# Normalising the rows of a mixture layer on GpSimd in place of VectorE

## The reference

```python
x = x + 0.5 * ffn(layernorm(x), ...)
x = x + attn(layernorm(x), ...)
x = x + 0.5 * ffn(layernorm(x), ...)

def layernorm(x, eps=1e-05):
    m = mean(x, axis=-1); v = var(x, axis=-1)
    return (x - m) / sqrt(v + eps)

def ffn(x, ...):                      # 8 experts of width 128, 2 per row, and one shared
    scores = sigmoid(x @ gate_W) * route_scale
    topk_scores, topk_idx = top_k(scores, 2)
    gate_full = ...                   # weights topk_scores / sum, scattered to 8 places
    h = gelu(einsum('bsd,edh->bseh', x, W1) + b1)
    y = einsum('bseh,ehd->bsed', h, W2) + b2
    return einsum('bse,bsed->bsd', gate_full, y) + gelu(x @ Ws1 + bs1) @ Ws2 + bs2
```

## Time and profile before

| | before |
|---|---|
| three timed executions | 2427.08, 2432.66, 2438.47 us, median 2432.66 |
| profiled execution | 2441.92 us, span 2440.1 us |
| TensorE busy | 2388.6 us, 98% of the span |
| VectorE busy | 1865.7 us, 76% |
| ScalarE busy | 1681.6 us, 69% |
| GpSimd busy | 1512.4 us, 62% |
| TensorE in the chain that ended last | 88% of the span |

### The profile page before, as it was taken

The page is one execution under the profiler, slowest core; times in us unless marked ns, Lnnn a source line. Parts: engine busy times, 40 slices in busy tenths (PEclk is TensorE's granted clock), DMA queues, the critical chain, the costliest instruction groups (busy, mean ns, idle before and its releaser), DMA issues.

```text
span 2440.1 us, 46268 instructions
## 1 busy us (share of the span) xinstructions
PE 2388.6 (98%) x14472; PEld 2078.3 (85%) x14472; DVE 1865.7 (76%) x3615; ACT 1681.6 (69%) x2932; POOL 1512.4 (62%) x1536
## 2 busy tenths in 40 slices
PE   8999889999999999999999999999999989999999
PEld 7888778888888888888888888888888879988888
DVE  7887567878888787887878888787887865466675
ACT  4555567878778787887878778787787865443443
POOL 1333267787877878777787777878777754542220
PEclk9999889999999999999999999999999999999999
DMA  4744531213222122321213222122221345432332
GB/s 179 264 162 163 198 113 38 94 47 100 73 74 95 44 86 71 93 95 43 86 57 95 75 67 95 44 86 78 86 95 43 108 157 166 140 115 64 126 130 82
DMA packets 131969, 245.66 MB, mean 101 GB/s; under 512 B 7290, under 2 KB 90132, under 8 KB 120052
## 3 DMA queue, kind: packets, MB, share of 16 engines
q1 hardware_dynamic: 131828, 244.15, 30.7%
HBM read 140.12 MB, written 53.67 MB: 79 GB/s over the span
## 4 chain that ended last, share of the span: by engine, by line
PE 88%; DVE 6%; DMA 2%; issue 1%; ACT 1%; POOL 1%; SPq 0%; DVEq 0%; ACTq 0%; POOLq 0%
PE a_sc L1661 19%; PE a_ov L1697 19%; PE a_tr L1673 18%; PE a_pj L1613 7%; PE a_pj L1620 4%; PE g_acc L963 3%; PE g_hid L921 3%; PE m_proj L2102 3%; PE f_acc L963 2%; PE f_hid L921 2%; PE m_hid L2168 2%; PE m_acc L2139 2%; DMA f_xin<-in_x 1%; DVE f_hp L735 1%; DVE f_gated L730 1%
## 5 line engine op out<-in xcount | busy, mean ns | idle before, releaser
L1569 DVE TENSOR_REDUCE a_nmax<-a_sc 128x1 f32<-128x1024 f32 x512 | 626.7, 1224 | 268.9 <-PE a_sc L1661 265.1
L1412 ACT ACTIVATE a_pT<-a_tr 128x512 fp32r<-128x512 f32 x1024 | 559.7, 596 | 324.2 <-PE a_tr L1673 321.4
L1496 POOL TENSOR_SCALAR a_pr<-a_pr,a_rden 128x1024 f32<-128x1024 f32 x512 | 576.7, 1127 | 294.6 <-DVE a_rden L1574 224.4
L1580 DVE TENSOR_TENSOR a_pT<-a_tr,a_pT 128x512 fp32r<-128x512 f32 x1024 | 650.0, 676 | 15.9 <-ACT a_pT L1412 15.9
L1697 PE MATMUL a_ov<-a_pT,a_v_s 128*128 128x512 f32 x2048 | 598.4, 414 | 3.1 <-DVE a_half L1560 2.0
L1418 ACT ACTIVATE a_pr<-a_sc,a_nmax 128x1024 f32<-128x1024 f32 x512 | 573.9, 1121 | 28.3 <-DVE a_nmax L1569 26.2
L1661 PE MATMUL a_sc<-a_k_s,a_q_s 128*128 128x512 f32 x2048 | 559.3, 395 | 3.5 <-DMA a_k_s<-a_k_s 3.5
L1673 PEld LDWEIGHTS a_tr<-f_ident,a_pr 128*128 128x128 f32 x4096 | 476.6, 140 | 79.7 <-DVE a_pT L1580 6.2
L1673 PE MATMUL a_tr<-f_ident,a_pr 128*128 128x128 f32 x4096 | 537.5, 274 | 1.8 <-DVE a_pT L1580 1.8
L1661 PEld LDWEIGHTS a_sc<-a_k_s,a_q_s 128*128 128x128 f32 x2048 | 378.2, 189 | 79.9 <-DMA a_k_s<-a_k_s 3.7
L1697 PEld LDWEIGHTS a_ov<-a_pT,a_v_s 128*128 128x128 f32 x2048 | 347.0, 189 | 50.5 <-issue 4.7
(11 more groups left out here) (252 smaller groups left out, 3228.4 us busy)
## 6 DMA issues: line engine op xcount, KB each, us to landing
a_z_s<-zT SPq DMA_DIRECT2D x32, 1024.0 KB, 7.7
a_k_s<-a_k_s SPq DMA_DIRECT2D x62, 512.0 KB, 5.6
a_wqk_s<-w_split SPq DMA_DIRECT2D x64, 256.0 KB, 3.2
a_v_s<-a_v_b SPq DMA_DIRECT2D x16, 1024.0 KB, 4.7
att<-a_ao SPq DMA_DIRECT2D x32, 512.0 KB, 2.9
m_in<-att SPq DMA_DIRECT2D x16, 1024.0 KB, 6.1
f_gB<-f_gate_rows SPq DMA_DIRECT2D x12, 1024.0 KB, 5.0
g_gB<-g_gate_rows SPq DMA_DIRECT2D x12, 1024.0 KB, 4.7
```

Of the source, the lines that this page charges most:

```text
L1412: act.activation(pT[:, (u // 4) % 2, 0, 4 * part:4 * part + 4, (u % 4) * P:(u % 4 + 1) * P], tr[:, part].rearrange("p (t q) -> p t q", t=4 ...
L1496: pool.tensor_scalar(pr[:, k % NP], pr[:, k % NP], rden[:, k % NP:k % NP + 1], 1.0, ALU.mult, ALU.mult).then_inc(s["normed"], 1)
L1569: dve.tensor_reduce(nmax[:, k % NP:k % NP + 1], sc[:, k % 2], AX.X, ALU.max, negate=True).then_inc(s["negmax"], 1)
L1580: dve.tensor_tensor(to[:, 1], tr[:, part].rearrange("p (t q) -> p t q", t=4), to[:, 0].bitcast(F32), ALU.subtract).then_inc(s["tr_lo"], 1)
```

## The change

`x_norm` goes from VectorE's stream to GpSimd's, for blocks 1 to 7 of both parts; block 0 stays on VectorE. On GpSimd it stands directly behind the `x_rstd` of the same block. It is the same operation on the same tiles, four instructions for a block, 28 for a part and 56 in all. Its waits are for GpSimd's own `rs` and for TensorE's transposes of the block before. `stand_alone` is a semaphore increment without work.

```diff
+        def x_norm(i, par):
+            pool.wait_ge(s["rstd"], i + 1)
+            pool.wait_ge(s["xT_ps"], i * DC)
+            stand_alone(pool, turns)
+            for t in range(NT):
+                o = pool.tensor_scalar(xn[:, t], xin[:, par, t], mv[:, t, 0:1], rs[:, t:t + 1], ALU.subtract, ALU.mult)
+            o.then_inc(s["xn"], 1)
...
             if first:
                 x_rstd(1)
+                x_norm(1, 1)
...
             if has(i, 2):
                 x_rstd(i + 2)
+                x_norm(i + 2, par)
...
                     if now("stats", e, first):
                         x_stats(i + 1, 1 - par)
-                    if now("norm", e, first):
-                        x_norm(i + 1, 1 - par, False)
...
                     if e == 6:
                         x_stats(i + 2, par)
-                    if e == 7:
-                        x_norm(i + 2, par, False)
```

## The result

| | before | after |
|---|---|---|
| median of 13 executions each | 2432.66 us (2427.08 to 2439.76) | 2447.26 us (2441.93 to 2457.02) |
| profiled execution, span | 2441.92, 2440.1 us | 2449.18, 2447.4 us |

The change made the kernel slower: ratio 1.0064, 95% interval 1.005 to 1.0078, that is some 15.6 us. The forecast was 2434 with a range up to 2443, and "slower" had a chance of 0.05. The prediction was wrong in its time, and in saying that the kernel would stay as fast as it was.

What follows compares the result with a forecast made beforehand. Both mixture parts were taken to run at TensorE's pace. Block 1 (+0.5 +0.5), block 2 (+0.3 -0.45 +1.0 -0.45) and later blocks (+0) summed to +1.4 us on the median 2432.66: 2434, range 2426 to 2443.

Steps and rivals of the forecast that it cites:

- the price of the moved instruction: One normalisation on GpSimd was taken at 404 ns, from a constant-operand row, with 0.76 us from an add as upper bound.
- The rival of the slow form: Two per-partition operands make GpSimd's instruction slow; above 1.2 us TensorE waits in later blocks; 35 us, 2468, chance 0.04.
- a room of 4.9: Later blocks, first part: 4.9 us between the deviations being ready and TensorE's transposes of `xn`, for a group of four.
- Its 5 us for each block 2: At 1.6 us an instruction, blocks 2 lose about as much as blocks 1 (5 us each), through held VectorE steps.
- +0.5 in each part: Block 1: one hold of GpSimd by VectorE delays `xn`, for which TensorE already waits; +0.5 us, ends 0 and 0.52.
- -0.45 twice: Block 2, prepared at the end of block 0: TensorE's 0.45 us wait for VectorE's low part goes, once in each part.
- +0.3: Block 2, first part: one GpSimd instruction holds the small VectorE steps ahead of `gpad`; +0.3 us, ends 0 and 1.4.
- +1.0: Block 2, second part: all four normalisations fall between the small steps ahead of `gpad`; +1.0 us, ends 0 and 1.4.
- worth 0: Blocks 3 to 7 of each part: relieving VectorE moves gating and low part earlier at most, nobody waits; 0 us.
- signs of being wrong: L595 over 1.2 us, TensorE waiting for `xn` in later blocks, or its waits for `hp` there shrinking.
- The meetings: GpSimd and VectorE hold each other on their SBUF path, up to the rest of an instruction; rival: cost nothing, -0.9 us, chance 0.2.
- about 23: VectorE's busy time over the kernel was to fall by about 23 us, counted as 56 x 407 ns.

Runs made afterwards that it cites:

- the first two experiments: The changed kernel with each block's four GpSimd normalisations in four forms, varying operands, then operations (output not the reference's); one execution took 2435.96 us, then 2435.16.
- the last experiment: The changed kernel with block 1 back on VectorE and blocks 2 to 7 on GpSimd as x * rs + shift; 2436.16 us, ratio 1.0012 to the kernel before.
- the shadow run: The kernel before, with 28 subtracting GpSimd instructions added on a tile nobody reads, first part alone; 2433.06 us, ratio 1.0006.
- the warm version: The changed kernel with 34 identity transposes filling TensorE's wait at block 1 of each part; 2449.37 us, then 2447.70 against 2452.31 for the change.

## Why the prediction was wrong

**The step that failed** is the price of the moved instruction: "I take the first, since one tensor is read", 404 ns, with 0.76 us as the bound from above. It measured 1216 ns, 0.8 us over the value and 0.45 over the bound. The bound was no bound, because the row behind it was of another operation. The nearest row had the engine, the size and the kind of instruction right and two multiplications where the change has a subtraction, and the first two experiments show that this makes some 670 of the 810 ns; the operands, which the prediction weighed instead, make the rest at 70 ns each. No row of the kernel before could tell: its only `tensor_scalar` instructions of this size on GpSimd multiply, and its `tensor_tensor` subtraction (741 ns) would have pointed the wrong way. The exception that it took from the Trainium skill (GPSIMD Engine Reference, "Engine selection": with one input GpSimd is about as fast) holds for multiplication and addition with constants (404 to 410 ns, for VectorE's 407), roughly with two operands (542 to 558), and not for subtraction, with 1068 to 1228 ns.

**The rival of the slow form** was the right structure under the wrong name. It said that TensorE waits in the later blocks from 1.2 us for one instruction, and block 1 pays in full. At 1.216 us eight of the ten later blocks wait, 0.16 to 1.11 us, and at 1.068 us none. At block 1 its rule gives 4 x 1.216 - 1.4 = 3.5 us, and 3.80 and 3.65 were measured. It was given 0.04, and its time of 35 us stood for 1.6 us an instruction. At the real price, with 5.19 us for a group in a room of 4.9, its rule makes 2 x 3.5 for block 1 and 10 x 0.3 for the later blocks, 10 us of the 15.6; most of the rest is the clock. Its 5 us for each block 2 had no ground: there the sum is a small gain (below).

**Block 1, "+0.5 in each part"**: +3.80 and +3.65 of wait. The reasoning, no slack, so all is passed on, was right, and the run with block 1 put back shows it: 13 us of the loss lie there. What no term of the sum had is the lower clock behind the wait, 2.3 and 2.7 us by the trace. A wait of this length costs more than itself.

**Block 2, "-0.45 twice", "+0.3", "+1.0"**: the two waits of 0.45 went. `gpad` came 0.43 and 0.27 us later: the first as said, the second a quarter of what I took. From `gpad`'s transposes to those of `xn` it takes 3.32 for 4.02 and 3.61 for 4.03, so block 2 in sum gained 0.3 and 0.15.

**Later blocks, "worth 0"**: the relief alone is worth 0.95 us in the first part and 0 in the second (the last experiment), so this reading was right within 1 us. But one of its signs of being wrong came true beside the other two (L595 over 1.2 us, and waits for `xn` in later blocks): TensorE's waits for `hp` did shrink, 16 us into blocks 3 to 6. The prediction looked only at the low part right behind the group and at the wait nearest to it; VectorE's backlog reached into the next block. The loss of 2.53 and 1.83 there is the price again. The room of 4.9 us was read rightly: a group of 5.19 us just exceeds it.

**The meetings**: holds go both ways as the earlier trace rows had it (gating 0.94 for 0.69, single normalisations up to 2292 ns), as the Trainium skill has it too (SBUF — State Buffer, "Who interferes with whom"): an exclusive lock on the port pair that the two engines share. Their cost was 0.7 us in the first part, by the shadow run, and was not what made the kernel slower.

**VectorE's busy time** fell by 14.8 us and not by "about 23". That figure counted 56 x 407 ns, while busy time counts overlapping instructions once: 14 x 1.38 = 19.3 was to be expected, and VectorE was held for part of the rest.

## What to carry to other kernels

A row prices an instruction only if it has the same engine, the same kind of instruction and the same arithmetic: neither `tensor_scalar` with a multiplication (404 ns) nor `tensor_tensor` with a subtraction (741) told of `tensor_scalar` with a subtraction (1068 to 1228); where the arithmetic differs, keep a bound wide enough to cross the point where the work no longer fits its room. When work moves to another engine, find first the one place where somebody already waits for it, and leave it there: here 8 of 56 instructions made some 13 of 15.6 us. And before moving work off an engine that looks busy, find what the relief is worth behind each piece: 19 us of VectorE were worth 1 to 2 (0.95, and the two waits of 0.45).

## What the runs showed of the hardware that I had not expected

GpSimd's `tensor_scalar` over 128x256 fp32 takes 404 to 410 ns with constants, 478 with one per-partition operand and 542 to 558 with two, if it multiplies and adds; with a subtraction in either place it takes 1068 to 1228 ns, while a `tensor_tensor` subtraction of that size takes 741. VectorE takes 407 for the very same subtraction and multiplication.

TensorE's granted clock fell to 0.50 behind waits of 2.1 to 4.4 us, and not each time. In all traces together, behind the waits of 3.6 to 4.4 us for `xn` it fell 6 times of 6; behind those of 2.1 to 2.7 us for `xn` or `gpad`, 5 times of 17. The same wait for `gpad` (2.26 and 2.25 us) had it in one execution of the warm version and not in the other. Of the waits of 2.1 to 2.7 us for `xn`, the three in second parts all had it and the three in first parts did not; why is not shown. Each time some 1.2 to 2.7 us went into the transposes and matmuls right behind the wait. The Trainium skill (TensorE: Matmul & The Clock Gate, "Part 1: The HAM clock gate") says that the clock halves after idling and that the number of slow matmuls varies from run to run. These rows agree with both: 0.50 behind 4.36 us of wait, and behind the same wait for `gpad` a first layer of 2.62 us in one execution and of 1.63 in the other. At the start of attention there is a longer fall. The windows there of the kernel before, then of the changed one:

```profile
290.00:300.00 10.00, 7.04 (x29) 6.66 (x30) 2.71 (x4) 2.31 (x4) 2.97 (x6) 0.60 0.79 252
300.00:310.00 10.00, 10.00 (x40) 9.23 (x41) 4.35 (x12) 1.82 (x4) 4.86 (x9) 0.50 0.00 0
```

```profile
290.00:300.00 10.00, 6.18 (x31) 4.47 (x29) 5.86 (x9) 6.09 (x9) 4.57 (x7) 1.00 0.53 156
300.00:310.00 10.00, 9.85 (x74) 9.32 (x74) 5.68 (x14) 3.38 (x6) 5.29 (x10) 1.00 0.51 161
```

In the one execution TensorE went through some 20 us at half its clock, in the other not, though the change touches nothing there. This is why the profiled executions differ by only 7.3 us: from the transposes of block 7 of the first part to those of block 0 of the second, the changed kernel's trace is 8.55 us the shorter. The timed executions vary likewise. Among the executions of the kernel before that were taken with the last version, nine took 2425.8 to 2430.0 us with a mean clock of 0.996 to 0.998, and eight 2435.2 to 2439.7 with 0.991 to 0.993; with the other runs the two groups are less clearly apart. Whether the same stretch makes that gap is not shown, since only one execution of each was profiled. The gap, some 5 us and more, is larger than most of what was studied here, and medians of a few executions move with how many fell on either side. What decides it between executions stays open.
